# A GNN and mixture-of-experts kernel: the one-hots of the second aggregation read their iota from PSUM

## The chip, the cores and the metric

The program runs on one core of a Trainium2 chip. The metric is the device time of one execution in microseconds; of several runs the median is given.

## The reference, cut to what matters

Four layers follow one another on 6250 nodes with 256 features: a graph layer with weighted edges, a small dense mixture, a second graph layer with edge attributes, and a routed mixture of eight experts. The change touches the third of them, where the attributes of each node's outgoing edges are averaged:

```python
src = edge_index[0]
sums = jax.ops.segment_sum(edge_attr, src, num_segments=n)
counts = jax.ops.segment_sum(jnp.ones((edge_attr.shape[0],), edge_attr.dtype), src, num_segments=n)
edge_attr_agg = sums / jnp.maximum(counts, 1.0)[:, None]
combined = jnp.concatenate([x, edge_attr_agg, u_expanded], axis=1)
h = jax.nn.relu(combined @ W1 + b1)
return h @ W2 + b2
```

There are 100000 edges, padded to 784 columns of 128. An edge row holds 64 attributes, a one (for the count) and the source node's number.

## The kernel before, in words

**Order of the stages.** First an aggregation by destination (the block whose TensorE part ends at line 687). Then a dense block, one loop over seven groups of seven node tiles (L968 and on). While it runs, GpSimd sorts the edges by source: `scatter` (L848 to L869) issues one indirect DMA per column of 128 edges from the stage buffer `front` to the DRAM tensor `sorted_edges` (L867). There are 784 such columns, 28 to a half of the stage buffer; SyncE refills a half (L805) once its scatters have landed, and the scatters go in batches of four on two alternating semaphores `s_sca`, so that a batch waits for the last but one to land. `behind_dense` ties some batches to points of the dense block, so that the scatter advances with it.

**The second aggregation.** The sorted edges are read back in runs of 512. An item is a pair of a run and a node tile; there are 292 items, in two segments. The first segment needs only edges among the first 504 columns, the second needs the rest. Per item:

- ScalarE's queue issues a load of the run, 512 rows, into one of 16 slots (`load`, L944 to L947). It waits until the product that used the slot before is done. Ahead of the first segment it waits for the scatters of `LANDED[0]` (L939), and between item 160 and the ones before it, at L956, for all 784 scatters (`LANDED[1]`).
- VectorE makes the one-hot, 128 x 512 (`onehots`, L1160 to L1165): a `scalar_tensor_tensor` that adds the tile's first number `tile_b` to an iota of 128 columns (repeated four times) and compares with the edges' source numbers. It writes one of 8 slots of `hot4`. Both inputs, `iota_r` and `rows4`, lie in SBUF.
- TensorE multiplies the rows with the one-hot (`products`, L1070 to L1076): four fp32 matmuls, which the trace shows as eight instructions, into one of 8 PSUM banks, `u % RING`.
- VectorE adds the bank, 65 x 128, to the tile's sum in SBUF (`add`, L1168 to L1172).

VectorE's order is written out: one-hot of item u + 4, then the sum of item u. TensorE's product of item u waits for its one-hot and, by `s_add`, for the sum that last used its bank, that of item u - 8. The semaphore `s_add` starts at `RING` = 8.

**After it.** When all items are summed (L806), the degrees are moved and turned, and the third block (L1309 and on) begins: the second graph layer's node part, routing, and the experts. The blocks follow one another on all engines.

**The first aggregation, for comparison.** It has the same one-hot (L562), whose iota `iota_p` lies in PSUM (copied there at L551); its edge numbers `dst_c` lie in SBUF. During it GpSimd issues 784 indirect gathers (L340). It has fewer banks for its products than slots for its one-hots: `bank` and `evicted` (L268 to L271) share two of them.

Of the kernel before, what the change touches and what calls it, by code (L numbers as in the profile page):

```python
# [6 lines left out]
P = 128  # L7
# [7 lines left out]
RUN = 4  # L15
# [15 lines left out]
STEP4 = 16  # L31
HALF4 = 4
# [20 lines left out]
EA = 64  # L53
ER = EA + 2
RING = 8
# [18 lines left out]
ALU = mybir.AluOpType  # L74
ACT = mybir.ActivationFunctionType
AX = mybir.AxisListType
ds = bass.ds
# [32 lines left out]
def build(nc, a, out):  # L110
# [7 lines left out]
    with ctx:  # L118
# [6 lines left out]
        psum = ctx.enter_context(nc.psum_tensor("psum", [P, 8, 512], f32))  # L125
        ident = sb("ident", [P, P])
        iota_r = sb("iota_r", [P, P])
# [572 lines left out]
        with ExitStack() as ph3:  # L700
# [30 lines left out]
            rows4 = spare[:, 0:STEP4 * RUN * ER].rearrange("p (u c f) -> p u c f", u=STEP4, c=RUN)  # L731
            tables = spare[:, STEP4 * RUN * ER:STEP4 * RUN * ER + 3 * NL].rearrange("p (n i) -> p n i", n=3)
            items4, tile_bi, tile_b = tables[0:2, 0, :].bitcast(i32), tables[:, 1, :].bitcast(i32), tables[:, 2, :]
            degrees = spare[0:NB, STEP4 * RUN * ER + 3 * NL:STEP4 * RUN * ER + 3 * NL + P]
            hot4 = h1[:, :, :].rearrange("p m n -> p (m n)")[:, 0:RING * RUN * P].rearrange("p (u c n) -> p u c n", u=RING, c=RUN)
            LANDED = tuple(tuple(sum(16 * EACH for b in range(c1 // EACH) if b % TURNS == turn) for turn in range(TURNS)) for c0, c1 in SEGMENTS)
            s_own4 = sem("later_vector_own")
            s_one = sem("l1_onehot_ready")
            s_prd = sem("l1_products")
            s_add = sem("l1_added")  # L740
# [34 lines left out]
            with nc.Block() as block:  # L775
# [187 lines left out]
                def _(pe):  # L963
# [4 lines left out]
                    with pe.Fori(0, NG) as g:  # L968
# [31 lines left out]
                        for r, ks in enumerate(FOURS):  # L1000
                            pe.wait_ge(s_y, g * 2 + r + 1)
                            for k in ks:
                                for c in range(2):
                                    at = k % 2 * D + c * P
                                    last = nc.tensor.transpose(psum[:, 4 + k // 2, at:at + P], xs[:, k, c * P:(c + 1) * P], ident[:, :])
# [21 lines left out]
                        for q in range(2):  # L1027
# [4 lines left out]
                            for n, (c0, c1) in enumerate(HALVES):  # L1032
                                for c in range(2):
                                    last = nc.tensor.matmul(psum[c * (P // 2):(c + 1) * (P // 2), 6 - 2 * q + n, 0:c1 - c0],
                                                            w2e[:, 2 * q + c, :], h1[:, 2 + 2 * q + c, c0:c1], start=True, stop=True)
                            last.then_inc(s_h2, 1)
                        pe.wait_ge(s_cf, g + 1)
                        for n, (c0, c1) in enumerate(HALVES):
                            for k in range(c0 // P, c1 // P):
                                last = nc.tensor.transpose(psum[0:5, n, k * P - c0:(k + 1) * P - c0], cf[:, k, :], ident[:, :])  # L1040
                        last.then_inc(s_cT, 1)
                        pe.wait_ge(s_cTc, g + 1)
                        for q in range(2):
                            for n, (c0, c1) in enumerate(HALVES):
                                last = nc.tensor.matmul(psum[:, 2 * q + n, 0:c1 - c0], pair[:, q, :], cfT[0:4, c0:c1], start=True, stop=True)
# [3 lines left out]
                        for ks in FOURS:  # L1049
                            for k in ks:  # L1050
                                there = psum[:, 4 + k // 2, k % 2 * D:(k % 2 + 1) * D]
                                for m in range(3):
                                    nc.tensor.matmul(there, h2[:, m, k * P:(k + 1) * P], w3[:, m, :], start=m == 0, stop=False)
                                last = nc.tensor.matmul(there, cfT[:, k * P:(k + 1) * P], b3[:, :], start=False, stop=True)
                            last.then_inc(s_y3, 1)
                        for r, ks in enumerate(FOURS):
                            pe.wait_ge(s_a5, g * 2 + r + 1)
                            for k in ks:
                                for c in range(2):
                                    at = k % 2 * D + c * P  # L1060
                                    last = nc.tensor.transpose(psum[:, k // 2, at:at + P], xs[:, k, c * P:(c + 1) * P], ident[:, :])
# [7 lines left out]
                    pe.sem_inc(s_prd, STEP4)  # L1069
                    def products(it, u):  # L1070
                        pe.wait_ge(s_one, it * STEP4 + u + 1)
                        pe.wait_ge(s_add, it * STEP4 + u + 1)
                        for c in range(RUN):
                            last = nc.tensor.matmul(psum[0:EA + 1, u % RING, 0:P], rows4[:, u, c, 0:EA + 1], hot4[:, u % RING, c, :],  # L1074
                                                    start=c == 0, stop=c == RUN - 1)
                        last.then_inc(s_prd, 1)  # L1076
                    with pe.Fori(0, ITS4) as it:
# [7 lines left out]
                def _(dve):  # L1085
                    dve.wait_ge(s_c3, 7)
                    nc.vector.tensor_copy(rev[:, :], rev_i[:, :]).then_inc(s_own3, 1)
                    with dve.Fori(0, NG) as g:
                        own = Chain(dve, s_own3, 1 + g * DENSE0_OWN)
# [4 lines left out]
                        for j, ks in enumerate(PAIRS):  # L1094
# [3 lines left out]
                            u = ks[0] % 4  # L1098
# [7 lines left out]
                        for k in range(G):  # L1106
                            x = xr[:, ds(g * G + k, 1), :].squeeze(1)
                            last = nc.vector.scalar_tensor_tensor(x, psum[:, k // 2, k % 2 * D:(k % 2 + 1) * D], rn[:, k:k + 1], x,
                                                                  ALU.mult, ALU.add)
# [43 lines left out]
                    own = Chain(dve, s_own4)  # L1153
# [2 lines left out]
                    own.add(nc.vector.memset(aggT[:, :, :], 0.0))  # L1156
                    dve.wait_ge(s_rst, 48)
                    own.add(nc.vector.tensor_scalar(tile_b[:, :], tile_bi[:, :], float(P), None, ALU.mult))
                    own.sync()
                    def onehots(it, u):  # L1160
                        dve.wait_ge(s_row4[u], it * 16 + 16)
                        dve.wait_ge(s_prd, STEP4 - RING + it * STEP4 + u + 1)
                        nc.vector.scalar_tensor_tensor(  # L1163
                            hot4[:, u % RING, :, :], iota_r[:, :].unsqueeze(1).to_broadcast([P, RUN, P]), tile_b[:, ds(it * STEP4 + u, 1)],
                            rows4[:, u, :, EA + 1:EA + 2].bitcast(i32).to_broadcast([P, RUN, P]), ALU.add, ALU.is_equal).then_inc(s_one, 1)  # L1165
                    for u in range(HALF4):
                        onehots(0, u)
                    def add(it, u, tile):  # L1168
                        dve.wait_ge(s_prd, STEP4 + it * STEP4 + u + 1)
                        dve.wait_ge(s_add, RING + it * STEP4 + u)  # L1170
                        there = aggT[:, ds(tile, 1), :].squeeze(1)
                        nc.vector.tensor_tensor(there, there, psum[0:EA + 1, u % RING, 0:P], ALU.add).then_inc(s_add, 1)  # L1172
                    def tiles_of(first):
                        return nc.values_load_multi_w_load_instructions(
                            items4[0:1, ds(first, HALF4)], [mybir.EngineType.DVE], min_val=0, max_val=NB - 1,
# [32 lines left out]
        with ExitStack() as ph6:  # L1208
# [100 lines left out]
            with nc.Block() as block:  # L1309
# [389 lines left out]
                def _(dve):  # L1699
# [93 lines left out]
                    places(NG - 2)  # L1793
                    gates(NG - 1)
                    places(NG - 1)
                    own = Chain(dve, s_own4, 4)
                    nc.vector.memset(zero8[:, 0:D], 0.0).then_inc(s_n7, 1)
                    nc.vector.memset(zero8[:, D + 1:ED], 0.0).then_inc(s_n7, 1)
                    own.add(nc.vector.tensor_scalar(part_f[:, :], part_i[:, :], 1.0, None, ALU.add))
# [139 lines left out]
```

## Time and profile before

| what | value |
|---|---|
| runs shown | 3382.25, 3386.84, 3408.57 us |
| median | 3386.84 us |
| span of the profiled execution | 3394.3 us |
| its own time | 3408.57 us, if it is one of the runs shown: the span is longer than the other two |
| what lies around its span | 14.3 us, by that reading |
| instructions | 46730 |
| mean granted TensorE clock | 0.863 |

The profiled execution was thus some 22 us slower than the median run. The span runs from the first instruction to the last; all times of rows are counted from its start. Durations below are those of that one execution. A DMA row on GpSimd is the time in which GpSimd writes the transfer's descriptors, not the transfer.

### The profile page before, as it was taken

The page shows a single profiled execution, that of the slowest core. Times are in us where ns is not written, and L with a number is a line of the kernel's source. Part 1 is how long each engine was busy: PE and PEld are TensorE (multiplying, and loading weights), DVE is VectorE, ACT ScalarE, POOL GpSimd, SP SyncE. Part 2 cuts the span into 40 slices and gives each one's busy share as a digit, 9 for nine tenths or more (in the row PEclk, how much of TensorE's full clock was granted, in tenths as well). Part 3 has the DMA queues.
Part 4 walks back from the last instruction along what each step waited for, and adds up shares of the span by engine and source line. Part 5 has one row for each costly group of instructions (what it writes and reads, how often), then busy time and mean ns, then how long its engine had stood idle before and what let it go on. Part 6 is the DMA issues. An engine that isn't in the chain of part 4 may idle for free. (4 is left out here: it accounts for less than half of the span.)

```text
span 3394.3 us, 46730 instructions
## 1 busy us (share of the span) xinstructions
PE 2566.3 (76%) x11173; PEld 1956.8 (58%) x11174; DVE 1344.0 (40%) x3191; ACT 934.7 (28%) x2174; POOL 1920.9 (57%) x1933
## 2 busy tenths in 40 slices
PE   0556566566665878778878879496995999999998
PEld 0434444444454554554544559495664888888775
DVE  6322227788832221221221259495562222222232
ACT  4655333333332222222222200001551111111222
POOL 4777777777776677777777778602245222222222
PEclk9877787888887777778787789798996999999999
DMA  6333334333333121121122146257344444444454
GB/s 211 99 105 104 104 104 127 105 104 104 104 104 93 46 80 52 66 81 61 57 76 73 50 145 169 72 157 193 134 140 150 112 108 109 109 109 109 134 163 133
DMA packets 206106, 369.66 MB, mean 109 GB/s; under 512 B 48133, under 2 KB 136686, under 8 KB 204143
## 3 DMA queue, kind: packets, MB, share of 16 engines
q0 software_dynamic: 83072, 157.64, 17.9%
q1 hardware_dynamic: 78348, 157.58, 14.1%
q10 hardware_dynamic: 44644, 53.97, 5.4%
q8 instruction: 15, 0.25, 0.0%
q14 instruction: 27, 0.22, 0.0%
HBM read 287.07 MB, written 81.97 MB: 109 GB/s over the span
## 5 line engine op out<-in xcount | busy, mean ns | idle before, releaser
L867 POOL DMA_INDIRECT sorted_edges<-front x768 | 819.9, 1068 | 278.2 <-issue 225.9
L340 POOL DMA_INDIRECT rows<-xn_rows,idx x784 | 748.0, 954 | 248.2 <-issue 225.5
L672 PE MATMUL psum<-rows,shared 128*128 x1984 | 609.9, 471 | 353.1 <-ACT rows L407 340.3
L672 PEld LDWEIGHTS psum<-rows,shared 128*128 128x128 f32 x1984 | 455.4, 237 | 507.6 <-issue 428.1
L407 ACT ACTIVATE rows<-rows,w_c 128x256 f32<-128x256 f32 x784 | 333.9, 496 | 578.9 <-DMA rows<-xn_rows,idx 578.9
L1074 PE MATMUL psum<-h,acc 128*65 128x128 f32 x2336 | 265.9, 276 | 67.3 <-DVE h L1163 67.3
L1074 PEld LDWEIGHTS psum<-h,acc 128*65 128x65 f32 x2336 | 257.2, 139 | 76.4 <-DVE h L1163 74.2
L1649 PE MATMUL psum<-xr 128*128 128x256 f32 x1344 | 300.0, 382 | 1.0 <-DVE xr L1860 1.0
L1660 PE MATMUL psum<-fw,xr 128*128 x1344 | 297.0, 379 | 0.0
L1649 PEld LDWEIGHTS psum<-xr 128*128 128x128 f32 x1344 | 257.4, 192 | 36.9 <-DVE xr L1860 1.4
L574 DVE TENSOR_TENSOR acc<-acc,psum 128x256 f32 x248 | 103.5, 417 | 424.5 <-PE psum L672 424.3
L1660 PEld LDWEIGHTS psum<-fw,xr 128*128 128x128 f32 x1344 | 252.1, 190 | 32.5
L1436 POOL DMA_INDIRECT out_y_dram<-xr,acc x84 | 130.7, 1556 | 237.5 <-ACT xr L1527 224.4
L1163 DVE SCALAR_TENSOR_TENSOR h<-iota_r,acc 128x512 f32<-128x512 f32 x292 | 217.2, 745 | 60.9 <-DMA acc<-sorted_edges 48.1
L562 DVE SCALAR_TENSOR_TENSOR shared<-psum,tile_b,dst_c 128x512 f32<-128x512 f32 x252 | 187.7, 746 | 42.2 <-issue 38.9
L988 PE MATMUL psum<-yT,w 128*128 128x512 f32 (+1 forms) x336 | 167.1, 661 | 19.3 <-ACT h L913 12.0
L1401 POOL DMA_INDIRECT dispatched<-acc,id x98 | 95.2, 971 | 137.2 <-DVE id L1773 109.2
L1869 DVE TENSOR_SCALAR xr<-psum,fb 128x256 f32<-128x256 f32 x168 | 73.5, 479 | 243.9 <-PE psum L1649 243.9
L1527 ACT ACTIVATE xr<-xr,acc 128x256 f32<-128x256 f32 x84 | 42.6, 508 | 344.1 <-DVE xr L1875 344.1
L1427 POOL COPY acc<-acc 128x18 f32<-128x18 f32 x43 | 8.6, 201 | 225.4 <-DVE xr L1860 225.4
L988 PEld LDWEIGHTS psum<-yT,w 128*128 128x128 f32 x336 | 76.3, 234 | 100.2 <-issue 64.0
L1875 DVE TENSOR_TENSOR xr<-psum,acc 128x256 f32<-128x256 f32 x84 | 35.7, 425 | 220.8 <-PE psum L1660 220.8
(314 smaller groups left out, 3237.0 us busy)
## 6 DMA issues: line engine op xcount, KB each, us to landing
xr<-in_f_W_dram SPq DMA_DIRECT2D x66, 1024.0 KB, 5.0
acc<-sorted_edges ACTq DMA_DIRECT2D x292, 132.0 KB, 2.2
front<-in_attr_dram SPq DMA_DIRECT2D x28, 924.0 KB, 4.7
rows<-xn_rows,idx POOLq DMA_INDIRECT x784, 2.7
sorted_edges<-front POOLq DMA_INDIRECT x784
hidden_parts<-h ACTq DMA_DIRECT2D x7, 1792.0 KB, 5.9
hx<-hidden_parts SPq DMA_DIRECT2D x7, 1792.0 KB, 8.2
h<-dispatched SPq DMA_DIRECT2D x42, 265.0 KB, 2.7
```

What stands on the lines that cost most here:

```text
L340: pool.indirect_dma_start(out=rows[:, c, :], out_offset=None, in_=xn_d, in_offset=bass.IndirectOffsetOnAxis(ap=idx[:, c:c + 1], axis=0)).t ...
L407: last = nc.scalar.activation(row, row, ACT.Copy, scale=w_c[:, ds((it * SLOTS + u) * RUN + c, 1)])
L562: nc.vector.scalar_tensor_tensor(hot[:, u, :, :], iota_p.unsqueeze(1).to_broadcast([P, RUN, P]), tile_b0[:, ds(i, 1)], dst_c[:, ds((run - ...
L574: nc.vector.tensor_tensor(there, there, psum[:, bank(u), 0:D], ALU.add).then_inc(s_acc, 1)
L672: last = nc.tensor.matmul(psum[:, bank(u), 0:D], hot[:, u, c, :], rows[:, ds(slots[k] + c, 1), :].squeeze(1), start=c == 0, stop=c == RUN - 1)
L867: pool.indirect_dma_start(out=edges_d, out_offset=bass.IndirectOffsetOnAxis(ap=sidx[:, h, c:c + 1], axis=0), in_=stage[:, h, c, :], in_off ...
L988: last = nc.tensor.matmul(psum[:, bank + n, 0:c1 - c0], w(c), x(c)[:, c0:c1], start=c == 0, stop=c == 1)
L1074: last = nc.tensor.matmul(psum[0:EA + 1, u % RING, 0:P], rows4[:, u, c, 0:EA + 1], hot4[:, u % RING, c, :], start=c == 0, stop=c == RUN - 1)
L1163: nc.vector.scalar_tensor_tensor(hot4[:, u % RING, :, :], iota_r[:, :].unsqueeze(1).to_broadcast([P, RUN, P]), tile_b[:, ds(it * STEP4 + u ...
L1436: pool.indirect_dma_start(out=out["y"], out_offset=bass.IndirectOffsetOnAxis(ap=wide_meta[:, u, h, 0:1].bitcast(i32), axis=0), in_=wide_y[ ...
L1649: last = nc.tensor.matmul(psum[:, 1 + m // 2, m % 2 * W:(m % 2 + 1) * W], wide_w[:, u, c, m * P:(m + 1) * P], wide_xT[:, c, :], start=c == ...
L1660: last = nc.tensor.matmul(psum[:, 5 + h, 0:D], wide_hT[:, m, h * P:(h + 1) * P], fw2[:, ds(e, 1), m, :].squeeze(1), start=m == 0, stop=m = ...
```

## The change

The iota is copied once into the first 128 columns of bank 7 of PSUM, and the one-hots of the second aggregation read it there. The products use banks 0 to 6: item u takes bank u % 8, and where that would be 7, bank 3 (`HALF4` is 4). Items with u % 8 of 3 and of 7 share bank 3, so their products wait for the sum of the item four before them, not eight. The semaphore count of the chain `own` behind the aggregation rises by one for the copy.

```diff
@@ build
+            iota4 = psum[:, RING - 1, 0:P]
+            def bank4(u):
+                return u % RING if u % RING < RING - 1 else u % RING - HALF4
+            def freed4(u):
+                return u + 1 + HALF4 if bank4(u) == RING - 1 - HALF4 else u + 1
@@ TensorE, products
-                        pe.wait_ge(s_add, it * STEP4 + u + 1)
+                        pe.wait_ge(s_add, it * STEP4 + freed4(u))
-                            last = nc.tensor.matmul(psum[0:EA + 1, u % RING, 0:P], rows4[:, u, c, 0:EA + 1], hot4[:, u % RING, c, :],
+                            last = nc.tensor.matmul(psum[0:EA + 1, bank4(u), 0:P], rows4[:, u, c, 0:EA + 1], hot4[:, u % RING, c, :],
@@ VectorE, ahead of the one-hots
+                    own.add(nc.vector.tensor_copy(iota4, iota_r[:, :]))
@@ VectorE, onehots
-                            hot4[:, u % RING, :, :], iota_r[:, :].unsqueeze(1).to_broadcast([P, RUN, P]), tile_b[:, ds(it * STEP4 + u, 1)],
+                            hot4[:, u % RING, :, :], iota4.unsqueeze(1).to_broadcast([P, RUN, P]), tile_b[:, ds(it * STEP4 + u, 1)],
@@ VectorE, add
-                        nc.vector.tensor_tensor(there, there, psum[0:EA + 1, u % RING, 0:P], ALU.add).then_inc(s_add, 1)
+                        nc.vector.tensor_tensor(there, there, psum[0:EA + 1, bank4(u), 0:P], ALU.add).then_inc(s_add, 1)
@@ VectorE, third block
-                    own = Chain(dve, s_own4, 4)
+                    own = Chain(dve, s_own4, 5)
```

On VectorE, at the start of the aggregation (L1163 and `h<-iota_r,acc` before are L1169 and `h<-psum,acc` in the changed kernel; `acc` holds the edge rows, the tables and the sums, `h` the one-hots). Before:

```order
476 L1156 MEMSET acc 65x6400 [waits l1_part_moved,l0_normalised]
477 L1158 TENSOR_SCALAR acc<-acc 128x292 [waits item_tables_moved]
478 L1163 SCALAR_TENSOR_TENSOR h<-iota_r,acc 128x512 [waits l1_products,l1_rows_loaded0,later_vector_own]
479 L1163 SCALAR_TENSOR_TENSOR h<-iota_r,acc 128x512 [waits l1_products,l1_rows_loaded1]
480 L1163 SCALAR_TENSOR_TENSOR h<-iota_r,acc 128x512 [waits l1_products,l1_rows_loaded2]
```

and now:

```order
476 L1161 MEMSET acc 65x6400 [waits l1_part_moved,l0_normalised]
477 L1163 TENSOR_SCALAR acc<-acc 128x292 [waits item_tables_moved]
478 L1164 COPY psum<-iota_r 128x128
479 L1169 SCALAR_TENSOR_TENSOR h<-psum,acc 128x512 [waits l1_products,l1_rows_loaded0,later_vector_own]
480 L1169 SCALAR_TENSOR_TENSOR h<-psum,acc 128x512 [waits l1_products,l1_rows_loaded1]
```

One copy stands ahead of the first one-hot, and each one-hot has one input in PSUM. The rest of VectorE's order is the same.

On TensorE, the products of items 2, 3 and 4 of the loop's 16. Before:

```order
362 L1074 MATMUL psum<-h,acc 65x128 [waits l1_added,l1_onehot_ready]
363 L1074 MATMUL psum<-h,acc 65x128 x3
364 L1071 REGISTER_ALU
365 L1074 MATMUL psum<-h,acc 65x128 [waits l1_added,l1_onehot_ready]
366 L1074 MATMUL psum<-h,acc 65x128 x3
367 L1071 REGISTER_ALU
368 L1074 MATMUL psum<-h,acc 65x128 [waits l1_added,l1_onehot_ready]
```

and now:

```order
362 L1079 MATMUL psum<-h,acc 65x128 [waits l1_added,l1_onehot_ready]
363 L1079 MATMUL psum<-h,acc 65x128 x3
364 L1076 REGISTER_ALU
365 L1077 REGISTER_ALU [waits l1_onehot_ready]
366 L1079 MATMUL psum<-h,acc 65x128 [waits l1_added]
367 L1079 MATMUL psum<-h,acc 65x128 x3
368 L1076 REGISTER_ALU
```

The matmuls stand in the same order; at one item in four the wait for the one-hot has moved to a register instruction, since the count for `l1_added` is another one. No order changes on ScalarE, GpSimd or SyncE.

## Rows read from the trace of the kernel before

**Rows 1.** The page, part 5: costliest groups (columns as the page's text says).
```profile
L867 POOL DMA_INDIRECT sorted_edges<-front x768 | 819.9, 1068 | 278.2 <-issue 225.9
L340 POOL DMA_INDIRECT rows<-xn_rows,idx x784 | 748.0, 954 | 248.2 <-issue 225.5
...
L1163 DVE SCALAR_TENSOR_TENSOR h<-iota_r,acc 128x512 f32<-128x512 f32 x292 | 217.2, 745 | 60.9 <-DMA acc<-sorted_edges 48.1
```
**Rows 2.** Who waited for whom between 1990 and 2325 us.
```profile
PEld psum L1074 <- DVE h L1163: 74.2, 29, 47.8
...
DVE h L1163 <- DMA acc<-sorted_edges: 48.1, 2, 47.7
...
DVE h L1163 <- PE psum L1074: 8.9, 18, 0.6
```
**Rows 3.** Timeline, 2190 to 2198 us: start, us, instruction.
```profile
2191.65 0.96 POOL L867 DMA_INDIRECT sorted_edges<-front  x1 [0.30 <-issue]
2194.86 3.23 ACTq L946 DMA_DIRECT2D acc<-sorted_edges  x6
2197.17 0.75 DVE L1163 SCALAR_TENSOR_TENSOR h<-iota_r,acc 128x512 f32<-128x512 f32 x1 [47.72 <-DMA acc<-sorted_edges]
```
**Rows 4.** Line 867 in three windows: 1600 to 1950, 2003 to 2149, 2150 to 2200 us.
```profile
L867 POOL DMA_INDIRECT sorted_edges<-front x269: 953/959/982, 1599.0 to 1949.9; - x135
...
L867 POOL DMA_INDIRECT sorted_edges<-front x52: 962/3180/3376, 2002.0 to 2146.8; - x52
...
L867 POOL DMA_INDIRECT sorted_edges<-front x34: 954/959/3257, 2146.8 to 2191.7; - x34
```
**Rows 5.** Lines 1163, 1172 and 1074 over the whole trace, and 1163 in 2000 to 2150 us.
```profile
L1163 DVE SCALAR_TENSOR_TENSOR h<-iota_r,acc x292: 739/743/802, 2000.9 to 2318.0; 128x512 f32<-128x512 f32 x146
...
L1163 DVE SCALAR_TENSOR_TENSOR h<-iota_r,acc x160: 739/742/802, 2000.9 to 2148.5; 128x512 f32<-128x512 f32 x160
...
L1172 DVE TENSOR_TENSOR acc<-acc,psum x292: 273/277/284, 2004.2 to 2320.6; 65x128 f32 x146
...
L1074 PE MATMUL psum<-h,acc x2336: 272/273/478, 2001.7 to 2319.6; 128*65 128x128 f32 x195
```
**Rows 6.** The first aggregation: lines 340, 562 and 551, all of the trace.
```profile
L340 POOL DMA_INDIRECT rows<-xn_rows,idx x784: 949/954/1207, 68.8 to 1059.3; - x196
...
L562 DVE SCALAR_TENSOR_TENSOR shared<-psum,tile_b,dst_c x252: 742/746/753, 102.9 to 1076.2; 128x512 f32<-128x512 f32 x126
...
L551 DVE COPY psum<-iota_r x1: 294/294/294, 100.7 to 100.7; 128x128 f32<-128x128 f32 x1
```
**Rows 7.** VectorE's timeline: a loop's turn, and the end of the first segment.
```profile
2015.46 0.74 DVE L1163 SCALAR_TENSOR_TENSOR h<-iota_r,acc 128x512 f32<-128x512 f32 x1
...
2016.56 0.75 DVE L1163 SCALAR_TENSOR_TENSOR h<-iota_r,acc 128x512 f32<-128x512 f32 x1
...
2147.65 0.74 DVE L1163 SCALAR_TENSOR_TENSOR h<-iota_r,acc 128x512 f32<-128x512 f32 x1
...
2148.51 0.74 DVE L1163 SCALAR_TENSOR_TENSOR h<-iota_r,acc 128x512 f32<-128x512 f32 x1
2149.17 0.28 DVE L1172 TENSOR_TENSOR acc<-acc,psum 65x128 f32 x1
```
**Rows 8.** Windows: length, busy (x count), clock; VectorE one-hots, then TensorE while it lags.
```profile
2060.95:2075.72 14.77, 11.91 (x16) 1.00 0.60 159
...
2203.17:2217.14 13.97, 13.97 (x131) 1.00 0.73 203
```
**Rows 9.** Windows: length, busy of PE, PEld, DVE, ACT, POOL, clock, DMA share, GB/s.
```profile
2026.00:2149.00 123.00, 120.27 (x1072) 115.64 (x1070) 117.34 (x267) 0.00 (x0) 109.79 (x42) 1.00 0.56 154
...
2150.00:2193.00 43.00, 0.44 (x5) 0.20 (x2) 0.00 (x0) 0.00 (x0) 31.94 (x35) 0.54 0.08 26
```

## The prediction, made before the changed kernel ran

> **What bounds the kernel now.** I read the page first, then the waits of the stage that the change touches, then the timeline around its longest wait, then the lines that meet there.
>
> The page's costliest groups show two lists of indirect DMAs on GpSimd, nearly equal in count, with the scatter at a mean of 1068 ns and the gather at 954 ns [rows 1]. The same view shows the one-hot of the second aggregation, 217.2 us busy, and before it 60.9 us of idle time, 48.1 of them ended by a load of sorted edges. The list of waits puts nearly all of that into one wait of 47.7 us [rows 2]. Everything else that VectorE waits for in the stage is 8.9 us in 18 pieces.
>
> The timeline says what that wait is [rows 3]. GpSimd starts its last scatter at 2191.65 and ends it at 2192.61. ScalarE's queue issues the first load of the second segment at 2194.86, since it stands behind the wait for all 784 scatters. The load lands and the one-hot of item 160 starts at 2197.17, after 47.72 us in which VectorE and TensorE did nothing. That idle stretch is on the path to the end: the third block waits for the last sum, and no other engine has work that outlasts it (43 us of the gap show TensorE with 0.44 us busy and ScalarE with none [rows 9]).
>
> Why is the scatter so late? Line 867 in three windows gives it [rows 4]. In the dense block, and again once VectorE stands still, an indirect DMA takes 958 or 959 ns. Between 2003 and 2149 us, while VectorE makes one-hots, its median is 3180 ns. Nothing of the scatter changed, only its neighbour. That neighbour reads two operands from SBUF, iota and edge rows. The gathers of the first aggregation, beside a one-hot of the same shape whose iota lies in PSUM, have a median of 954 ns and a maximum of 1207 [rows 6]. So the rows tie the stall to the second SBUF input.
>
> The Trainium skill (SBUF — State Buffer, section "Who interferes with whom") states this as a rule: a VectorE instruction with two SBUF inputs contends with a GpSimd instruction that reads SBUF, and with one SBUF input it does not. By that rule, the trace agrees: 3180 ns against 954. The same section also holds a sentence against the change: it infers that such an instruction takes only the read side, that writing descriptors needs the write side, and that this is why a plain `tensor_tensor` was not seen to stall a DMA. By this the scatter would stay as slow as it is and the time would not move; the row of 3180 ns speaks against it, and the third rival below carries it.
>
> **The change part by part.**
>
> *The scatter beside the one-hots.* From 2002.0 to its end there are 85 scatters: 52 in one window and 34 in the next, with the one at 2146.8 in both [rows 4]. Once VectorE is idle, a scatter takes 0.96 us with 0.30 us of idle before it [rows 3, 4], that is 1.26 us. In the dense block 269 of them span 1599.0 to 1949.9, 1.31 us each with their waits [rows 4]. The best case for the changed kernel is 85 x 1.26 = 107 us, an end at 2109; with the dense block's pace 85 x 1.31 = 111 us, at 2113. The worst is that nothing improves. I take 1.31, since its loads of the stage buffer and its waits for landings are real. All edges are then there at about 2115.
>
> *The wait at item 160.* Item 160's one-hot would come, with no wait, one step behind the last ones of the first segment. These start at 2148.51, with the sum of item 155 at 2149.17 [rows 7]; the step from one one-hot to the next is 0.86 within a group of four and 1.10 at a loop's turn (2015.46 to 2016.56), where item 160 stands, so it would start at about 2149.6 rather than 2197.17. Its load must be issued some 2.3 us earlier (2194.86 to 2197.17 [rows 3]), so anything before 2147 will do, and the scatter beats this by 32 us. It would meet it even at a pace of (2147 - 2002) / 85 = 1.7 us. So the relief need not be complete; this is why I trust the term more than any of its parts. The gain is 2197.17 - 2149.6 = 47.6 us, and no more: what the scatter finishes early beyond that buys nothing, because VectorE's own pace is next.
>
> *The pace after it.* What is late next is VectorE. Sixteen items take 14.77 us of it, of which the one-hots are 11.91, and the sums, partly beside them, and the loop's register loads the rest. TensorE, when it lags and works without a pause, needs 13.97 us for the same 16 [rows 8]. TensorE's 2336 instructions are 8 an item, and both segments hold the same forms [rows 5]. The pace is thus VectorE's, 0.92 us an item, and stays so.
>
> *The one-hot from PSUM.* Its duration: 743 ns now [rows 5], 746 ns for the same form with a PSUM iota [rows 6]. That is 3 ns x 292 = 0.9 us on the path. The bounds are the two minima (742 against 739, the same 3 ns) and nothing at all; I take 0.9. The Trainium skill (VectorE: DVE Perf Modes, section "The TRN2 errata") gives VectorE a fixed part of 58 cycles from SBUF and 120 from PSUM; its 62 cycles of difference would be an estimated 65 ns, 19 us over 292 items. The rows show 3 ns for a mixed pair, so I weigh it as nearly nothing.
>
> *The copy of the iota.* It takes 294 ns [rows 6] and stands between the table and the first one-hot, where nothing covers it: 0.3 us, with 0.2 and 0.4 as ends.
>
> *Seven banks.* Of each 16 items four, those with u % 4 = 3, now wait for the sum of four items earlier. VectorE's order is one-hot (u), then sum (u - 4). The sum starts 0.66 us behind the one-hot's start and takes 0.28 [rows 7], so it is done 0.94 us behind that start. The one-hot itself is done at 0.74. A TensorE that keeps up will thus start such a product about 0.2 us later than it does. That falls out of its slack: it has 14.77 - 13.97 = 0.80 us a turn, exactly what four waits of 0.2 would use. They do not add up in truth, for each wait is measured against VectorE's clock and not against TensorE's last item. VectorE needs a product only at its sum, four items or 3.7 us behind its one-hot, while the product takes TensorE 0.87 us (13.97 / 16) once the one-hot is there. So the price is 0. With a TensorE that is already behind, as in the first items, the sum in question is long done. The upper end is that each of 73 products costs the 0.2 us: 15 us. What hides it is VectorE's pace; were VectorE 5% faster, this would show.
>
> *More DMA at one time.* The first segment's share of the DMA engines is 0.56 with 42 scatters in 123 us; scatters alone take 0.08 at 35 in 43 us [rows 9]. At full pace the sum is about 0.65. A load lands in 2 to 3 us and is issued up to 16 items ahead, so I price this at 0, with 3 us as the upper end.
>
> *The sum.* -47.6 + 0.9 + 0.3 = -46.4 us. Against the profiled execution this is 3394.3 - 46.4 = 3347.9 us of span, or 3362.2 with the 14.3 us around it. That execution was 22 us above the median run, and none of the terms depends on where those 22 us were spent, so against the median: 3386.8 - 46.4 = 3340.4 us, 1.4% less.
>
> **The rivals.**
>
> *TensorE in step with VectorE (slower than before).* If the shared bank really holds TensorE, and it restarts only when the sum is seen, each fourth product could cost a whole pair of one-hot and sum, about 1.0 us of standing. Four items of TensorE take 13.97 / 4 = 3.49; with it 4.49 against VectorE's 3.69, so 0.80 x 73 = 58 us more. The gain is then turned round: 3340.4 + 58 = 3399 us. For it speaks that TensorE is only 5% faster than VectorE. Against it speaks that the sum is done 0.2 us behind the one-hot that TensorE waits for anyway. It begins to cost at a stall of 0.20 us per fourth product and outweighs the gain at 0.20 + 46.4 / 73 = 0.84.
>
> *A part of the stall is a cost (faster, by less).* The 15 us of the upper end above, or a one-hot slower by some 50 ns (50 ns x 292 = 15 us): 3355 us. The rows on the one-hot speak against the second.
>
> *The relief does not come.* The scatter stays at 3180 ns, as it would if the sums (which read one SBUF operand) or the writes of the one-hots hold it: the wait at item 160 stays, and 1.2 us are added: 3388 us. The gathers of the first aggregation speak against it, with sums and one-hots of the same forms beside them. Half a relief, at up to 1.7 us a scatter, would still give the whole gain.
>
> **How the numbers follow.** The forecast has 0.82, the partial cost 0.10, no relief 0.06, the step-lock 0.02. The predicted time is 3340.4. Below it I leave room for a run that is itself quicker by what the runs shown differ, down to 3330; above it the range takes in most of the partial cost, to 3354. A measurement of this kernel can tell about 1% from no change, 34 us, so the bound is 3353. Faster by over 1% holds the forecast and a little of the partial cost, less the chance that the runs scatter by the 0.8% of those shown: 0.83. Within 1%: 0.15. Slower by over 1%: 0.02.
>
> **What the profile of the changed kernel would show.** Right: scatters beside the one-hots at a median near 960 ns, the last one at about 2110; no wait of VectorE for a load longer than a microsecond; one-hots at 746 ns; the last sum near 2274 instead of 2320.6 [rows 5]; TensorE waiting a little oftener for VectorE's sums, 0.2 us each; the span near 3348 if the rest runs as in the profile of before. Wrong: a median of the scatter still over 1.7 us with a wait at item 160; VectorE's 16 items over 14.9 us, with waits for products ahead of its sums; or a third block that begins 46 us earlier but lasts longer.

## The result and the profile after

The changed kernel took 3332.73 us (median of 4 runs, 3328.6 to 3357.46) against 3384.64 us before: a ratio of 0.984, with a 95% interval of 0.981 to 0.987. Forecast were 3340.4 us and a gain of 46.4 us; measured were 51.9.

The profiled execution took 3328.60 us with a span of 3326.9, so 1.7 us lie around a span. The 14.3 us that I read for the kernel before were wrong: its profiled execution must have taken some 3396 us and is none of the three runs listed. It thus lay some 9 us above the median run, and not 22 as the prediction has it. The forecast against the median uses neither number.

The page of the changed kernel, costliest groups (L872 was L867, L1079 was L1074, L1169 was L1163):

```profile
L872 POOL DMA_INDIRECT sorted_edges<-front x768 | 739.0, 962 | 275.3 <-issue 226.1
L340 POOL DMA_INDIRECT rows<-xn_rows,idx x784 | 747.6, 954 | 248.2 <-issue 224.3
...
L1169 DVE SCALAR_TENSOR_TENSOR h<-psum,acc 128x512 f32<-128x512 f32 x292 | 216.8, 744 | 13.1 <-PE psum L1079 9.6
```

The scatter's mean went from 1068 to 962 ns and the idle time ahead of the one-hots from 60.9 to 13.1 us [rows 1]. Who waited for whom in the stage, 1980 to 2290 us:

```profile
PEld psum L1079 <- DVE h L1169: 22.4, 17, 15.7
...
DVE h L1169 <- PE psum L1079: 9.6, 19, 0.6
PEld psum L1079 <- DVE acc L1178: 5.1, 31, 0.2
...
DVE h L1169 <- DMA acc<-sorted_edges: 0.2, 1, 0.2
```

The wait of 47.7 us for a load [rows 2] is gone. A new kind of wait has come, TensorE's weight load for a sum: 31 times, 0.2 us at most. The lines themselves, over the whole trace, with line 872 in the window of 2003 to 2149 us first:

```profile
L872 POOL DMA_INDIRECT sorted_edges<-front x82: 954/958/979, 2002.3 to 2106.5; - x82
...
L1169 DVE SCALAR_TENSOR_TENSOR h<-psum,acc x292: 739/741/752, 1994.2 to 2262.7; 128x512 f32<-128x512 f32 x146
...
L1178 DVE TENSOR_TENSOR acc<-acc,psum x292: 271/274/284, 1997.5 to 2265.3; 65x128 f32 x146
...
L1164 DVE COPY psum<-iota_r x1: 277/277/277, 1993.9 to 1993.9; 128x128 f32<-128x128 f32 x1
```

Beside the one-hots a scatter's median is 958 ns, where it was 3180, and its maximum 979, where it was 3376 [rows 4]. The last one starts at 2106.5. VectorE passes item 160 without a pause:

```profile
2141.26 0.74 DVE L1169 SCALAR_TENSOR_TENSOR h<-psum,acc 128x512 f32<-128x512 f32 x1
2141.92 0.28 DVE L1178 TENSOR_TENSOR acc<-acc,psum 65x128 f32 x1
2142.34 0.75 DVE L1169 SCALAR_TENSOR_TENSOR h<-psum,acc 128x512 f32<-128x512 f32 x1
```

The step at 2142.34 is item 160: 1.08 us (forecast 1.10) instead of 48.66 (2148.51 to 2197.17 [rows 3, 7]). From the first one-hot to the last the aggregation takes 268.5 us instead of 317.1 [rows 5]: 48.6 us less.

### The profile page after: what moved, and what is told of

It reads as the page before. It is cut to its first block and busy times, and to the rows that moved or that the text cites. A ratio compares the mean times of both kernels' runs of the same rounds, so it can differ in the third digit from the quotient of the medians.

```text
span 3326.9 us, 46677 instructions
## 1 busy us (share of the span) xinstructions
PE 2556.9 (77%) x11173; PEld 1947.4 (59%) x11174; DVE 1343.0 (40%) x3192; ACT 934.2 (28%) x2174; POOL 1838.5 (55%) x1933
## 5 line engine op out<-in xcount | busy, mean ns | idle before, releaser
L872 POOL DMA_INDIRECT sorted_edges<-front x768 | 739.0, 962 | 275.3 <-issue 226.1
L1079 PE MATMUL psum<-h,acc 128*65 128x128 f32 x2336 | 266.9, 276 | 18.0 <-DVE h L1169 17.9
L1079 PEld LDWEIGHTS psum<-h,acc 128*65 128x65 f32 x2336 | 255.1, 138 | 30.2 <-DVE h L1169 22.4
L1169 DVE SCALAR_TENSOR_TENSOR h<-psum,acc 128x512 f32<-128x512 f32 x292 | 216.8, 744 | 13.1 <-PE psum L1079 9.6
```

The source lines that it names most:

```text
L872: pool.indirect_dma_start(out=edges_d, out_offset=bass.IndirectOffsetOnAxis(ap=sidx[:, h, c:c + 1], axis=0), in_=stage[:, h, c, :], in_off ...
L1079: last = nc.tensor.matmul(psum[0:EA + 1, bank4(u), 0:P], rows4[:, u, c, 0:EA + 1], hot4[:, u % RING, c, :], start=c == 0, stop=c == RUN - 1)
L1169: nc.vector.scalar_tensor_tensor(hot4[:, u % RING, :, :], iota4.unsqueeze(1).to_broadcast([P, RUN, P]), tile_b[:, ds(it * STEP4 + u, 1)], ...
```

## The experiments

There were twelve runs in four sets, each set on a chip of its own. On two of these chips the kernel before takes 3880 us instead of some 3390; they are called the slower chips, and what they showed is told below. A stage can be read on any chip from its own trace.

**The changed kernel once more.** No edit.

> The changed kernel once more, for a second profile and a time on the chip of its neighbours. My theory (the gain is the wait at item 160, about 48 us, and nothing outside the second aggregation) expects 48 us less than the kernel before, 0.986 of it, and an aggregation of 271 us from the first one-hot to the last sum. The rival (a part of the 52 us between the medians comes from other blocks) expects 52 us again, 0.984, with the aggregation still at 271 us and the third block some 4 us shorter than that of the kernel before.

Measured: 0.987 of the kernel before, interval 0.983 to 0.992, so 43 us with room from 27 to 58. Its first and last one-hot start at 1995.6 and 2264.4, 268.8 us apart. So the aggregation gives 48.6 us each time, and both ratios hold that. Whether the other 3 us of the first comparison are real stays open: the interval around it is 10 us to each side.

**Seven banks alone, iota in SBUF.**

```diff
-    hot4[:, u % RING, :, :], iota4.unsqueeze(1).to_broadcast([P, RUN, P]), ...
+    hot4[:, u % RING, :, :], iota_r[:, :].unsqueeze(1).to_broadcast([P, RUN, P]), ...
```

> The products use seven banks as in the changed kernel, the copy of the iota stays, but the one-hots read the iota from SBUF. Theory: the time of the kernel before within 3 us (ratio 1.000), scatters at a median near 3.2 us, a wait of 47 us at item 160, and TensorE starting one product in four 0.1 us later. Rival (the shared bank costs 0.2 us for each of 73 products): 15 us slower than before, ratio 1.004. Rival (the gain comes from the banks or the order, not from the iota): 50 us faster than before.

Measured: ratio 1.0016, interval 0.9997 to 1.0035. In its trace the scatter (2003 to 2149 us) and the longest wait of the stage are:

```profile
L872 POOL DMA_INDIRECT sorted_edges<-front x52: 954/3182/3372, 2002.9 to 2147.9; - x52
```
```profile
DVE h L1169 <- DMA acc<-sorted_edges: 49.0, 1, 49.0
```

The stall of the scatter and the wait are both back, so the iota's place makes the whole gain. The interval alone would leave room for a cost of the banks of up to 12 us; the stage does not: from its first to its last one-hot it takes 318.6 us (1993.9 to 2312.5) with a wait of 49.0, against 317.1 with 47.7 before.

**The iota of every second one-hot from SBUF.**

```diff
-    iota4.unsqueeze(1)
+    (iota4 if u % 2 else iota_r[:, :]).unsqueeze(1)
```

> The changed kernel, with the iota of every second one-hot read from SBUF. Theory: in the kernel before a scatter of 0.96 us needs 3.7 steps of VectorE, 0.26 us of progress for each one-hot with two SBUF inputs; so half of them gives 0.86 + 0.26 = 1.12 us of progress in 1.72 us, 1.5 us a scatter and 1.8 us a step. 85 scatters then take 150 us and end just about where item 160 is due: the wait there is 0 to 8 us, the time 0 to 8 us above the changed kernel. Rival (GpSimd is slowed by what the one-hots write or by the sums, or the relief needs every one-hot): scatters near 3 us, a wait over 40 us, the time of the kernel before.

**Three of four from SBUF.**

```diff
-    iota4.unsqueeze(1)
+    (iota4 if u % 4 == 3 else iota_r[:, :]).unsqueeze(1)
```

> The changed kernel, with the iota of only one one-hot in four read from PSUM, three from SBUF. Theory: progress of 0.86 + 3 x 0.26 = 1.64 us in 3.69 us, so 2.15 us a scatter and 2.45 us a step; 60 of 85 are issued when the first segment is done, 25 at 1.26 us are left, and the wait at item 160 is about 35 us: 35 us above the changed kernel, 13 below the kernel before. Rival (the stall depends on whether any such one-hot overlaps a scatter at all): scatters near 3.2 us and a wait of 47 us.

Measured: 0.987 (0.983 to 0.992) and 0.984 (0.980 to 0.988). Neither has a wait at item 160, and their one-hots take 270.3 and 270.8 us from first to last. Line 872 between 2003 and about 2149 us in the second of them:

```profile
L872 POOL DMA_INDIRECT sorted_edges<-front x83: 954/1072/2336, 2002.3 to 2139.2; - x83
```

The first expectation named the right end (no wait), but its median is 960 ns, not 1500, and its step 1.46 us, not 1.8. The second was wrong by 35 us: 83 scatters start in 137 us, 1.67 us a step instead of 2.45, which is just under the 1.7 us that I had worked out as enough. One free one-hot in four gives all of the gain but some 2 us. So a stalled scatter does not advance a little in each gap, as my sum of 0.26 us for each one-hot had it. GpSimd's timeline in the same kernel, then VectorE's (spans on GpSimd are rough):

```profile
2058.01 2.01 POOL L872 DMA_INDIRECT sorted_edges<-front  x1 [0.30 <-issue]
2060.32 0.96 POOL L872 DMA_INDIRECT sorted_edges<-front  x1 [0.30 <-issue]
2061.59 2.10 POOL L872 DMA_INDIRECT sorted_edges<-front  x1 [0.31 <-issue]
2063.99 0.96 POOL L872 DMA_INDIRECT sorted_edges<-front  x1 [0.30 <-issue]
```
```profile
2059.30 0.74 DVE L1169 SCALAR_TENSOR_TENSOR h<-psum,acc 128x512 f32<-128x512 f32 x1
...
2060.39 0.75 DVE L1169 SCALAR_TENSOR_TENSOR h<-iota_r,acc 128x512 f32<-128x512 f32 x1
...
2061.25 0.74 DVE L1169 SCALAR_TENSOR_TENSOR h<-iota_r,acc 128x512 f32<-128x512 f32 x1
...
2062.97 0.74 DVE L1169 SCALAR_TENSOR_TENSOR h<-psum,acc 128x512 f32<-128x512 f32 x1
```

The scatter that starts at 2060.32, 0.07 us ahead of a one-hot with two SBUF inputs, takes its 0.96 us as if nothing were there. The one that starts at 2061.59, in the middle of such a one-hot, ends 0.72 us after the next PSUM one-hot has begun. The reading is that a scatter waits to begin and then runs through.

The trace of the kernel before bears this out. GpSimd's rows there, then VectorE's:

```profile
2072.97 3.24 POOL L867 DMA_INDIRECT sorted_edges<-front  x1 [0.31 <-issue]
2076.52 3.36 POOL L867 DMA_INDIRECT sorted_edges<-front  x1 [0.31 <-issue]
```
```profile
2074.64 0.74 DVE L1163 SCALAR_TENSOR_TENSOR h<-iota_r,acc 128x512 f32<-128x512 f32 x1
...
2075.72 0.75 DVE L1163 SCALAR_TENSOR_TENSOR h<-iota_r,acc 128x512 f32<-128x512 f32 x1
...
2076.59 0.74 DVE L1163 SCALAR_TENSOR_TENSOR h<-iota_r,acc 128x512 f32<-128x512 f32 x1
```

The first scatter ends at 2076.21, 0.83 us behind the end of the one-hot at 2075.38. Of the 51 scatters that start there between 2004 and 2147 us, 50 take over 1 us, and each of the 50 ends 0.82 to 0.85 us behind the end of a one-hot, whether it was held by one of them or by three. Nearly its whole time thus still lies ahead of a held scatter when it is let in. The gaps between one-hots that held scatters passed over, 65 of them, are 0.12 us at most; they were let in 41 times at gaps of 0.15 us or more (the stop at item 160 is one), and 9 times at short ones. What decides at a short gap is not shown.

To start first is not enough. The scatter of 2076.52 starts 0.07 us ahead of the one-hot of 2076.59, but right behind the one before, and takes 3.36 us. All 9 scatters of the kernel before that stand so take 3.35 to 3.38 us. With three of four from SBUF, 16 scatters start 0.03 to 0.09 us ahead of a one-hot with two SBUF inputs: the 8 that follow a PSUM one-hot take 0.95 or 0.96 us, the 8 right behind a one-hot with two SBUF inputs 1.60 to 1.67.

The Trainium skill (SBUF — State Buffer, section "Who interferes with whom") says, of VectorE's modes that use both port pairs, that whoever issues first gets the shared pair for its whole instruction while the other blocks fully, and in general that the order of issue decides who blocks. That a held scatter is blocked fully, and not slowed, agrees with the 0.82 to 0.85 us. That the first to start wins does not: it fails in the 9 cases above, and the one-hot of 2060.39 is not blocked by a scatter that began before it (0.75 us, as ever).

**The same instructions, one-hots in pairs.** This tests that reading with all iotas in SBUF and eight banks. Both kernels of this set hold the scatter's last 84 columns back until the dense block's last store, so that they meet the aggregation on any chip:

```diff
+    if isinstance(g, int) and g == NG - 1 and q == 1:
+        pool.wait_ge(s_hx, NG * 16 + 1)
+        alone(pool)
...
-    with pool.Fori(1, NG) as g:
+    with pool.Fori(1, NG - 1) as g:
         scatter(g, False)
+    scatter(NG - 1, False)
```

(`alone` only counts up a semaphore of its own engine), and the second of them has VectorE's order changed, from one-hot, sum, one-hot, sum to one-hot, one-hot, sum, sum.

> The kernel before, with the last 84 columns of the scatter held back until the dense block's last store has landed, so that the aggregation always starts with some 80 of them left, on a chip where they would otherwise be done too. Theory (the wait at item 160 is what is left of the scatter after the first segment, at 2.8 us a step beside the one-hots): scatters beside the one-hots at a median near 3.2 us, a wait of 40 to 48 us at item 160. The time is 40 to 48 us above the kernel before where that has none left at the start of the aggregation (near 3880 us), and within 5 us of it where it has 85 left (near 3385 us). Rival (on the slower chip the scatter is not stalled by the one-hots at all): no wait there and the time of the kernel before.

> The kernel with the held scatter, iota in SBUF and eight banks, with VectorE's order changed from one-hot, sum, one-hot, sum to one-hot, one-hot, sum, sum: the same instructions, but after two one-hots some 0.6 us without a second SBUF input instead of 0.12 us after each. Theory A (a scatter is stalled only until it finds a gap long enough to begin, and is not held once it has begun): scatters at a median under 2 us, a step under 1.75 us, no wait at item 160, 40 us or more below the kernel with the held scatter. Theory B (a scatter is slowed in proportion to the time that VectorE holds a second SBUF input, which this order does not change): scatters near 3 us and the wait of 40 to 48 us stays.

Measured: the held kernel 0.9997 (0.998 to 1.001) of the kernel before, 3391.6 us, since this set ran on a faster chip again, with a wait of 51.5 us at item 160, where I had 40 to 48. Its rival, that the scatter is not stalled on a slower chip, could therefore not be tested. Its scatters between 2003 and 2149 us have a lower median than the 3.2 us expected, with the same longest ones:

```profile
L870 POOL DMA_INDIRECT sorted_edges<-front x54: 955/2772/3368, 2002.1 to 2148.8; - x54
```

The paired order: 3420.1 us, 1.007 of the kernel before (1.004 to 1.010). Its scatters and its waits between 2001 and 2150 us:

```profile
L870 POOL DMA_INDIRECT sorted_edges<-front x84: 957/962/1505, 2004.5 to 2120.3; - x84
```
```profile
DVE h L1167 <- issue: 10.4, 23, 0.6
DVE acc L1176 <- DVE acc L1176: 9.7, 46, 0.2
DVE h L1167 <- PE psum L1078: 6.8, 9, 0.9
...
DVE h L1167 <- DMA acc<-sorted_edges: 0.3, 1, 0.3
```

On the scatter theory A is right and B falls: 962 ns, a step of 115.8 / 83 = 1.40 us, no wait at item 160, with two SBUF inputs in every one-hot. On the time it is wrong by 68 us or more. A sum that follows a sum waits 0.2 us for its count (9.7 us in this window), and register work ahead of a one-hot seems to be laid bare (the 10.4 us of "issue"); the rest of the loss was not taken apart. VectorE's one-hots run from 2000.7 to 2340.7 instead of 1992.1 to 2312.5 in the held kernel: the wait of 51.5 us went and 71 us of pace came.

**Fewer banks.** On a slower chip, where no scatter is left when the aggregation begins.

```diff
-    return u % RING if u % RING < RING - 1 else u % RING - HALF4
+    return u % HALF4          # two banks: u % 2; one bank: 0
-    return u + 1 + HALF4 if bank4(u) == RING - 1 - HALF4 else u + 1
+    return u + 1 + HALF4      # two banks: u + RING - 1; one bank: u + RING
```

> The changed kernel with four banks for the products instead of seven: every product waits for the sum of the item four before it. Theory: in the changed kernel TensorE starts such a product 0.99 us behind the start of its one-hot instead of 0.89, and VectorE needs it only 3.7 us later; so every product starts at about 1.0 us, sixteen items still take 14.7 us, and the time is that of the changed kernel within 2 us. Rival (a stall of 0.2 us for each product adds to TensorE's 0.87 us and makes it the bound at 1.07 us): 0.15 x 292 = 44 us above the changed kernel.

> The changed kernel with two banks: every product waits for the sum of the item two before it. Theory: a product starts at the sum that stands behind the one-hot two items later, 2 x 0.86 + 1.0 = 2.7 us after its own one-hot, ends 1.03 us later at 3.75, and VectorE wants it at 4 x 0.86 + 0.67 = 4.1 us; it is just covered, and the time stays within 5 us of the changed kernel. Rival (the lock step of TensorE and VectorE costs as soon as banks are scarce): over 40 us above the changed kernel.

> The changed kernel with one bank: every product waits for the sum just before it. Theory: now product (1.03 us), sum (0.28 us) and two hand-overs of some 0.05 us follow one another, 1.4 us an item against 0.92; 292 x 0.48 = 140 us above the changed kernel, near 3470 us. Rival (TensorE and VectorE overlap in some other way): under 60 us above it.

Line 1169 over the trace of each, in that order:

```profile
L1169 DVE SCALAR_TENSOR_TENSOR h<-psum,acc x292: 741/741/752, 2501.0 to 2769.0; 128x512 f32<-128x512 f32 x146
```
```profile
L1169 DVE SCALAR_TENSOR_TENSOR h<-psum,acc x292: 741/741/753, 2500.3 to 2787.7; 128x512 f32<-128x512 f32 x146
```
```profile
L1169 DVE SCALAR_TENSOR_TENSOR h<-psum,acc x292: 741/751/753, 2499.6 to 2970.0; 128x512 f32<-128x512 f32 x146
```

Four banks: 268.0 us from the first to the last one-hot, as in the changed kernel, although every product now has to wait for the sum of the item four before; its time is 0.9994 (0.9974 to 1.0013) of the kernel before there. The ring of seven is free, and so is one of four. Two banks: 287.4, so 19 us more, where I had under 5 and the rival over 40; the time is 1.0047 (1.0023 to 1.0071). TensorE's weight loads wait for sums 34.7 us in 71 pieces, up to 0.9 us, instead of 11.6 in 31, and the idle time ahead of the one-hots that is put down to TensorE grows from 8.3 to 26.7 us. My cover of 0.35 us was too thin; which hand-over used it up is not shown. One bank: 470.4, so 202 us more (1.61 us an item), and 1.052 (1.046 to 1.058), where I had 140 us; right in kind, a third too small.

**The kernel before on a slower chip, and the changed one on the other.**

> The kernel before, for a second profile. Theory: the 12 us by which the third block is shorter in the profile of the changed kernel are the difference between two executions, so this profile has a third block of 1061 to 1068 us if its span is near 3382 us, and a wait of 47 us at item 160 whatever its span. Rival (the change shortens the third block): a third block of 1073 us again, with a span near 3394 us.

> The changed kernel beside the one with the early start, on the same chip. Both theories expect the kernel before less 50 us, 0.985.

Measured: the kernel before has a median of 3879.8 us on the first of the two and 3878.1 on the second, and the changed kernel there takes 1.0013 of it (0.9992 to 1.0034): no gain, where both theories had expected 0.985. The trace of the kernel before on the first, lines 867 and 1163:

```profile
L867 POOL DMA_INDIRECT sorted_edges<-front x768: 952/958/983, 1276.8 to 2485.5; - x192
```
```profile
L1163 DVE SCALAR_TENSOR_TENSOR h<-iota_r,acc x292: 739/742/754, 2507.2 to 2775.3; 128x512 f32<-128x512 f32 x146
```

The last scatter starts at 2485.5 and the first one-hot at 2507.2. They never meet (nor in the changed kernel on the other chip, 2478.3 and 2499.5), so nothing is stalled, there is no wait at item 160, and the one-hots take 268.1 us with their iota in SBUF. The stages before are longer there: from the first scatter to the first one-hot it is 1230 us, where it was 912 (1088.7 to 2000.9), 35% more. The scatter has slowed by less: 1208.7 / 767 = 1.58 us a column, where the 683 columns issued by 2000.9 took 1.34 each, 18% more. So it is through before the dense block ends. Whether the change would gain there if the two did meet was not tested.

What slows that chip is open. The first aggregation in windows (columns as in [rows 9]), on the chip of the first comparison and then there:

```profile
0.00:1090.00 1090.00, 624.50 (x2051) 465.12 (x2052) 547.74 (x976) 440.42 (x1127) 789.98 (x847) 0.83 0.38 112
```
```profile
0.00:1277.00 1277.00, 657.75 (x2051) 469.94 (x2052) 544.54 (x976) 446.11 (x1127) 788.16 (x846) 0.74 0.33 95
```

The granted clock is lower, 0.74 against 0.83, but TensorE is only 33 us busier in a stretch 187 us longer, and the other engines hardly differ: what is added is mostly idle time. The page puts it down to "issue" (595.2 us ahead of the weight loads below, 428.1 on the first chip) and to "remote", an unknown releaser:

```profile
L672 PEld LDWEIGHTS psum<-rows,shared 128*128 128x128 f32 x1984 | 459.4, 243 | 665.9 <-issue 595.2
...
L574 DVE TENSOR_TENSOR acc<-acc,psum 128x256 f32 x248 | 102.9, 415 | 543.5 <-remote 392.3
```

The question of the third block (12 us shorter in the first profile of the changed kernel) could not be read there, since the block is longer on that chip anyway. From the last one-hot to the end the faster chips' profiles give 1064.2 and 1063.5 us for the changed kernel, 1069.7 for three of four, 1068.7 for seven banks alone and 1068.1 for the held kernel, against 1076.3 before. The last two have the wait at item 160 and are 8 us shorter than the kernel before all the same, so most of the 12 us is a spread of executions; whether 4 us of it are real stays open.

**The aggregation begun earlier.** An attempt to improve on both kernels.

```diff
 @@ ScalarE, ahead of the table loads
-                    act.wait_ge(s_hx, NG * 16 + 1)
 @@ VectorE: this wait moves from ahead of the memset to ahead of the copy of the iota
+                    dve.wait_ge(s_hx, NG * 16 + 1)
                     own.add(nc.vector.tensor_copy(iota4, iota_r[:, :]))
```

> The changed kernel with the start of the aggregation moved ahead: ScalarE issues the loads of the tables and of the first runs without waiting for the store of the hidden parts, and VectorE clears the sums and makes its table ahead of that wait instead of behind it; only the copy of the iota and the one-hots, which overwrite what the store reads, stay behind it. The last copy of hidden parts and its store end at about 1987 us in the profile of the changed kernel, the clearing takes 5.39 us from 1988.41, the first one-hot starts at 1994.20. Theory: the first one-hot starts 5 to 6 us earlier behind the dense block, and the time is 5 to 6 us less than that of the changed kernel. Rival (the first loads compete with the store, or the edges sorted so far bind): 0 to 2 us less.

Measured: 3883.0 us against 3883.6 for the changed kernel beside it, no difference. In the trace, the last store's issue and what follows it:

```profile
2490.18 0.34 ACTq L937 DMA_DIRECT2D hidden_parts<-h  x1
2490.70 0.34 ACTq L939 DMA_DIRECT2D acc<-item_rows  x1
2491.08 1.22 ACTq L940 DMA_DIRECT2D acc<-item_rows  x1
2497.57 0.31 DVE L1161 TENSOR_SCALAR acc<-acc 128x292 f32<-128x292 int32 x1 [18.87 <-DMA acc<-item_rows]
...
2498.76 7.50 ACTq L950 DMA_DIRECT2D acc<-sorted_edges  x12
2500.97 2.82 DVE L1168 SCALAR_TENSOR_TENSOR h<-psum,acc 128x512 f32<-128x512 f32 x4 [2.88 <-issue]
```

The first one-hot comes 10.8 us behind the store's issue, where the changed kernel beside it has 12.9 (2486.54 to 2499.48). The table loads, issued right behind the store, land only some 6 us later. So the start gains 2.2 us, near the rival's 0 to 2, and no run can tell it.

## Why the prediction was right, point by point

- *The bound* (one wait of 47.7 us, its cause a scatter stalled by the second SBUF input): right, and shown. With the iota in SBUF and seven banks the stall and the wait return; with it in PSUM both go.
- *The wait at item 160*, -47.6 us: measured -47.58 (48.66 less 1.08).
- *The scatter's end*, about 2113, at 1.31 us a scatter: the last one started at 2106.5, with a step of 104.2 / 81 = 1.29 us.
- *The threshold of 1.7 us*: supported by the kernel with three of four from SBUF, which has 1.67 and the whole gain. It was the right thing to trust.
- *The one-hot from PSUM*, +0.9 us: nothing came of it. Its median is 741 ns in the first trace of the changed kernel and 743 in the second, against 743; sixteen items take 14.73 us instead of 14.77 [rows 8]. The 19 us that I had estimated from the Trainium skill (VectorE: DVE Perf Modes, section "The TRN2 errata") did not come, as the prediction had weighed it.
- *The copy*, 0.3 us: 0.277.
- *Seven banks*, 0: right. Such a product waits 5.1 / 31 = 0.16 us at times, not 0.2 at each. VectorE's sums waited for products for 1.6 us in all, against 0.9 before. Down to four banks it stays so, and no rival of 58 us lurked there. TensorE's slack is also a little more than the prediction has: the window of 13.97 us holds 131 instructions [rows 8], and 16 items are 128.
- *More DMA at one time*, 0: right, 0.2 us of waits for loads.
- *The sum*, -46.4 us: in the aggregation 48.6 less 0.3 for the copy ahead of it. What is over, up to 51.9, lies within what executions differ by. The two profiled executions differ by more, 67.4 us: 6.7 of them ahead of the first one-hot (2000.9 against 1994.2), 48.6 in the aggregation and 12.1 behind it. Only the 48.6 are explained by the change. That the profile's last sum (2265.3) and span (3326.9) fall below the forecast 2274 and 3348 is the rest of this.
- *The profiled execution*, 22 us above the median: misread, some 9 us. No term rests on it.
- *What I did not forecast* is how narrow the condition is. The prediction counted 85 scatters left at the start as a property of the kernel. It is one of that kernel on that chip: where the stages before run 25% longer (2507.2 against 2000.9 us), none is left, and no gain was measured.
- *How the stall works* was taken for a slowing in proportion in the expectations behind the prediction; the prediction itself needed only that the relief beats 1.7 us a scatter.

## What to carry to other kernels

When GpSimd issues indirect DMAs beside a back-to-back row of VectorE instructions with two SBUF operands, move one operand to PSUM, or see that every few microseconds a stretch without a second SBUF operand comes by; it need not be every instruction (one in four, every 3.7 us, was enough here). A reordering can make such stretches too, but here it cost 71 us of pace for a wait of 51.5. Before paying for it, ask when the delayed DMAs are needed: the value of the change is the wait at that point and no more, and it falls to nothing where the DMAs are through before the two meet. Sharing PSUM banks costs nothing as long as the reader comes several items behind the writer; work out that distance, and leave a margin: here a bank used again four items later was free, and with two items a computed cover of 0.35 us was not enough.

## What the runs showed of the hardware that I had not expected

- A scatter held by one-hots with two SBUF inputs is held whole and then runs through: 50 of 50 end 0.82 to 0.85 us behind the end of one. A gap of 0.12 us between them was passed over 65 times.
- A scatter's stall is not in proportion to the time that VectorE uses its second SBUF input. At 100%, 75%, 50% and 0% of the one-hots with two SBUF inputs, the median is 3180, 1072, 960 and 958 ns.
- The order of the same instructions decides as much as their operands: in pairs, with 0.7 us or more between the pairs, one-hots with two SBUF inputs leave the scatter at a median of 962 ns.
- The same kernel took 3385 to 3395 us on some chips and 3880 on two others, with the aggregation equal (268.1 us from the first to the last one-hot there, 268.5 without the wait here), 1104 us after it instead of 1064 to 1076, and 2507 us ahead of it instead of 2001.
